# A two-layer graph network on one core: one more tile of lag in the delta stage, and every fourth message pair summed in two halves

## What is computed

```python
def step(S, x):
    qt, kt, vt, bt, gt = x
    S = S * jnp.exp(gt)[..., None, None]
    kv = jnp.einsum('bhk,ebhkv->ebhv', kt, S)
    delta = (vt[None] - kv) * bt[..., None]
    S = S + kt[None, :, :, :, None] * delta[..., None, :]
    ot = jnp.einsum('bhk,ebhkv->ebhv', qt * scale, S)
    return (S, ot)
```

```python
msg = jax.nn.relu(x[src] + edge_attr @ W_e + b_e)
aggr = jax.ops.segment_sum(msg, dst, num_segments=x.shape[0])
```

## Time and profile before

| | |
|---|---|
| time, median of 3 runs | 3208.61 us (3206.28 to 3215.51) |
| profiled execution | 3215.71 us, span 3213.9 us |
| PE busy | 2905.2 us, 90% |
| DVE busy | 1669.4 us, 52% |
| POOL busy | 1488.0 us, 46% |
| ACT busy | 1136.8 us, 35% |
| chain that ended last | PE 74%, issue 10%, DVE 5%, ACT 4%, POOL 4%, DMA 2% |

### The profile page before, as it was taken

The page is one execution under the profiler, slowest core; times in us unless marked ns, Lnnn a source line. Parts: engine busy times, 40 slices in busy tenths (PEclk is TensorE's granted clock), DMA queues, the critical chain, the costliest instruction groups (busy, mean ns, idle before and its releaser), DMA issues.

```text
span 3213.9 us, 46196 instructions
## 1 busy us (share of the span) xinstructions
PE 2905.2 (90%) x16081; PEld 1658.6 (52%) x16081; DVE 1669.4 (52%) x3820; ACT 1136.8 (35%) x2501; POOL 1488.0 (46%) x1471
## 2 busy tenths in 40 slices
PE   6999999988899899858989898999999999999828
PEld 3433566667676644447777664444533333444424
DVE  7633355578344432268777643442267777521361
ACT  3312422289122222346666441220044444331201
POOL 0565756488654537633333204545566666200004
PEclk9999999999999999979999998999999999999959
DMA  5400001120111234434454454211176666500404
GB/s 173 140 19 5 7 25 49 46 71 16 32 52 44 72 121 165 166 104 126 117 143 128 136 148 159 77 53 38 49 227 199 198 205 190 156 0 27 183 0 132
DMA packets 275961, 321.38 MB, mean 100 GB/s; under 512 B 155807, under 2 KB 193569, under 8 KB 275732
## 3 DMA queue, kind: packets, MB, share of 16 engines
q1 hardware_dynamic: 219684, 182.57, 18.7%
q0 software_dynamic: 51840, 134.60, 13.4%
q10 hardware_dynamic: 4208, 1.25, 0.2%
HBM read 215.75 MB, written 104.60 MB: 100 GB/s over the span
## 4 chain that ended last, share of the span: by engine, by line
PE 74%; issue 10%; DVE 5%; ACT 4%; POOL 4%; DMA 2%; SPq 0%; ACTq 0%; POOLq 0%; DVEq 0%
PE bank L2730 8%; PE bank L1522 5%; PE bank L2722 5%; PE bank L708 4%; PE bank L1301 4%; PE bank L2393 3%; PE bank L2884 3%; PE bank L2877 3%; PE bank L439 3%; PE bank L731 2%; PE bank L762 2%; PE bank L1117 2%; PE bank L2373 2%; PE bank L1311 2%; PE bank L858 2%
## 5 line engine op out<-in xcount | busy, mean ns | idle before, releaser
L2702 POOL DMA_INDIRECT conv_src<-xn_rows,keep x288 | 272.9, 948 | 175.7 <-DVE conv_msg L2768 110.4
L291 POOL DMA_INDIRECT sorted_bias<-perf_rec,place x256 | 259.7, 1014 | 146.0 <-PE bank L708 91.6
L2730 PE MATMUL bank<-conv_msg,conv_hot 128*128 128x512 f32 x576 | 273.0, 596 | 0.6 <-ACT conv_msg L2749 0.6
L2768 DVE TENSOR_TENSOR conv_msg<-bank,conv_src 128x512 f32<-128x512 f32 x288 | 185.5, 686 | 47.2 <-PE bank L2722 47.2
L1936 POOL TENSOR_TENSOR delta_dec<-delta_dec,rates_of 128x512 f32<-128x512 f32 x64 | 68.8, 1075 | 282.5 <-ACT delta_dec L1988 282.5
L666 POOL DMA_INDIRECT sorted_edge<-rec,place x128 | 127.1, 993 | 141.4 <-PE bank L1362 75.0
L2749 ACT ACTIVATE conv_msg<-conv_msg 128x1024 f32<-128x1024 f32 x144 | 152.0, 1056 | 102.0 <-DVE conv_msg L2768 102.0
L1117 PE MATMUL bank<-bias_prod,bias_hot 128*128 128x256 f32 x640 | 148.2, 387 | 25.1 <-ACT bias_hot L1070 13.0
L2722 PE MATMUL bank<-conv_we,conv_eT 64*128 64x512 f32 x576 | 164.5, 648 | 0.7 <-ACT conv_eT L2746 0.7
L1101 POOL TENSOR_TENSOR bias_prod<-bias_col,bias_rec 128x512 f32<-128x512 f32 x128 | 147.2, 1179 | 16.4 <-PE bank L1117 15.7
L1117 PEld LDWEIGHTS bank<-bias_prod,bias_hot 128*128 128x128 f32 x640 | 120.1, 192 | 53.7 <-issue 28.1
(11 more groups left out here) (502 smaller groups left out, 6674.8 us busy)
## 6 DMA issues: line engine op xcount, KB each, us to landing
keep<-slot_qkv SPq DMA_DIRECT2D x32, 512.0 KB, 4.0
delta_kv<-slot_qkv SPq DMA_DIRECT2D x32, 512.0 KB, 3.9
sorted_edge<-sort_pad SPq DMA_DIRECT2D x8, 1440.0 KB, 7.4
keep<-sorted_edge SPq DMA_DIRECT2D x18, 640.0 KB, 4.8
slot_out<-delta_o SPq DMA_DIRECT2D x64, 128.0 KB, 2.2
conv_src<-xn_rows,keep POOLq DMA_INDIRECT x288, 3.6
X<-in_x SPq DMA_DIRECT2D x4, 1024.0 KB, 11.3
sorted_bias<-perf_rec,place POOLq DMA_INDIRECT x256
```

Source lines behind the costliest of these rows:

```text
L291: POOL.indirect_dma_start(out=sorted_bias, out_offset=bass.IndirectOffsetOnAxis(ap=place[:, 0, c:c + 1], axis=0), in_=rec0[:, c, :], in_of ...
L2702: POOL.indirect_dma_start(out=src[:, n % 4, j, :], out_offset=None, in_=xn_rows, in_offset=bass.IndirectOffsetOnAxis(ap=rec[:, g % 3, k + ...
L2730: a = PE.matmul(bank[n % 2][:, :], hot[:, g % 2, k + j, :], msg[:, q, j, :], start=j == 0, stop=j == 1)
L2768: DVE.tensor_tensor(msg[:, q, j, :], bank[2 + 2 * q + j][:, :], src[:, n % 4, j, :], ALU.add).then_inc(*raw.up())
```

## The change

In the delta stage the ring of key products holds ten tiles instead of nine, and the main part, the import of the inverses, and the constants FIRST, ALONE and TWO all move two chunks (one tile) later. To make room, `kv` has two buffers instead of three, `o` three instead of four, `kd`, `r` and `w` one instead of two, and a table `strict` is dropped. Each smaller ring adds a wait on the step that last read the buffer. The chain of 30 columns is spread over 7.3 chunks instead of 5.4; a column has two plan entries now, and where its product falls ahead of `BA`, its update is placed behind `BA`. `L copy` moves from 6.33 to 8.23 chunks after the batch begins. From chunk 18 on the high mask is made by ACT in four activations, between `Z copy` and `U copy`, and no longer by POOL.

In the message stage pairs with n % 4 == 1 are summed in halves: relu writes an fp32r tile `high`, DVE computes `low` = relu(msg) - high, and PE sums with four fp32r matmuls (two of `high`, two of `low`) in place of two f32 ones. `raw` is one instruction of 128x1024 for both tiles. `turn`, `eT`, `edge`, `raw`, `relu` and `gather` stand earlier in the plan; `pack` and `hot` stay.

```diff
-            R = 9
+            R = 10
-            MID, MAIN = 15.8, 17.2
-            ALONE, TWO, FIRST = 16, 14, 16
+            MID, MAIN = 17.8, 19.2
+            ALONE, TWO, FIRST = 18, 16, 18
-            kv = sb("kv", [P, 3, 2, D])
+            kv = sb("kv", [P, 2, 2, D])
-            strict = sb("strict", [P, 32 * 32])
-            kd, r_, w = (sb(n, [P, 2, HG, HD]) for n in ("kd", "r", "w"))
-            o = sb("o", [P, 4, HG, HD])
+            kd, r_, w = (sb(n, [P, HG, HD]) for n in ("kd", "r", "w"))
+            o = sb("o", [P, 3, HG, HD])
...
-                return (("mask", -0.45), ("turn", -0.35), ("kq", -0.25), ("low mask", 0.17), ("gram", 0.22), ("decay", 0.25),
+                return (("high mask", -0.1), ("turn", -0.35), ("kq", -0.25), ("low mask", 0.17), ("gram", 0.22), ("decay", 0.25),
...
-                plan.append((2 * t + (14.6 if t >= 2 else 13.6 + 0.4 * t), "UL in", t))
-                plan.append((2 * t + MAIN - 3.0, "load kv", t))
+                plan.append((2 * t + (16.6 if t >= 2 else 13.6 + 0.4 * t), "UL in", t))
+                plan.append((2 * t + MAIN - 2.6, "load kv", t))
...
-                    at = 0.75 + (5.4 if q else 3.0) * (31 - k) / 31
+                    at = 0.75 + (7.3 if q else 3.0) * (31 - k) / 31
...
-                    plan.append((first + int(at) + part, "block column", (q, k)))
-                plan.append((first + (6.33 if q else 5.19), "L copy", q))
-                plan.append((first + (6.34 if q else 5.2), "blocks out", q))
+                    plan.append((first + int(at) + part, "block product", (q, k)))
+                    plan.append((first + int(at) + (0.745 if q and part < 0.7 else part), "block update", (q, k)))
+                plan.append((first + (8.23 if q else 5.19), "L copy", q))
+                plan.append((first + (8.24 if q else 5.2), "blocks out", q))
...
+                    if what == "high mask":
+                        ACT.wait_ge(*decay_sum.at(n))
+                        for i, h in enumerate(range(g * HG, (g + 1) * HG)):
+                            a = ACT.activation(dec_half[:, 0, i, :], const("upto"), AF.Copy, scale=rate_half[:, 0, t, h:h + 1])
+                        a.then_inc(*masked.up())
...
+            high, low = (sb(n, [P, 2, 2, D], F32H) for n in ("high", "low"))
...
+                return n % 4 == 1
...
-                for what, at in (("gather", -3.6), ("turn", -2.3), ("eT", -2.2), ("edge", -1.75), ("raw", -1.4), ("relu", -0.85),
+                for what, at in (("gather", -3.9), ("turn", -3.05), ("eT", -2.9), ("edge", -2.15), ("raw", -1.8), ("relu", -1.25),
                                  ("sum", 0.0), ("add", 0.6)):
                     plan.append((n + at, what, n))
+                if in_halves(n):
+                    plan.append((n - 0.7, "low", n))
...
                         for j in range(2):
-                            a = PE.matmul(bank[n % 2][:, :], hot[:, g % 2, k + j, :], msg[:, q, j, :], start=j == 0, stop=j == 1)
+                            PE.matmul(bank[n % 2][:, :], hot[:, g % 2, k + j, :], high[:, n // 4 % 2, j, :], start=j == 0, stop=False)
+                        PE.wait_ge(*lowered.at(n // 4 + 1))
+                        for j in range(2):
+                            a = PE.matmul(bank[n % 2][:, :], hot[:, g % 2, k + j, :], low[:, n // 4 % 2, j, :], start=False,
+                                          stop=j == 1)
                         a.then_inc(*summed.up())
...
-                        for j in range(2):
-                            DVE.tensor_tensor(msg[:, q, j, :], bank[2 + 2 * q + j][:, :], src[:, n % 4, j, :],
-                                              ALU.add).then_inc(*raw.up())
+                        DVE.tensor_tensor(msg[:, q, :, :], pairs[1 + q][:, :, :], src[:, n % 4, :, :], ALU.add).then_inc(*raw.up())
+                    if what == "low":
+                        DVE.wait_ge(*active.at(n + 1))
+                        if n >= 8:
+                            DVE.wait_ge(*summed.at(n - 7))
+                        DVE.scalar_tensor_tensor(low[:, n // 4 % 2, :, :], msg[:, q, :, :], 0.0, high[:, n // 4 % 2, :, :].bitcast(F32),
+                                                 ALU.max, ALU.subtract).then_inc(*lowered.up())
```

More of the change, by code:

```diff
@@ L1966, in scalar @@
                         continue
-                    if what not in ("kq", "low mask", "exp", "Z copy", "U copy", "Zb copy", "T copy", "w"):
+                    if what not in ("kq", "high mask", "low mask", "exp", "Z copy", "U copy", "Zb copy", "T copy", "w"):
                         continue
@@ L2168, in vector @@
                             DVE.wait_ge(*L_ready.at(n))
-                        DVE.scalar_tensor_tensor(flat(Us), flat(Bs), -1.0, strict[:, :], ALU.mult, ALU.mult
-                                                 ).then_inc(*blocks.up())
+                        DVE.tensor_scalar(flat(Us), flat(Bs), -1.0, None, ALU.mult).then_inc(*blocks.up())
                         DVE.wait_ge(*blocks.now())
                         DVE.memset(flat(Us)[:, 0:32 * 32:33], 1.0).then_inc(*blocks.up())
-                    if what == "block column":
+                    if what == "block product":
                         q, k = n
@@ L2699, in pool @@
                         if n >= 4:
[L2700 removed]
+                            POOL.wait_ge(*raw.at(n - 3))
                         for j in range(2):
```

84 lines of the change are left out of this document (48 added, 36 removed).

## The result

The changed kernel takes 3187.49 us, the median of 9 runs (3185.25 to 3200.14). The kernel before, in 9 runs beside them, takes 3208.61 us (3205.72 to 3219.67). The ratio is 0.9939, with a 95% interval of 0.9923 to 0.9954: 0.6% faster, 21 us where 10.6 were forecast. The profiled execution of the changed kernel took 3185.78 us with a span of 3183.9 us, 30 less than before.

What follows compares the result with a forecast made beforehand. PE bounds the message stage; DVE's order sets five or six of eight steady delta chunks, PE with ACT the rest. Message -16 and delta +5.5 make -10.5 from the 3208.6 median: 3198 us, range 3189 to 3208 (eight in ten 3175 to 3216).

Steps and rivals of the forecast that it cites:

- rival 1: Delta stage: the DVE-POOL lock is worth all 0.7 us of DVE per chunk, 15 us in all: 3183 us; chance 0.16.
- Rival 2: Message stage: the pack is in time, so 13.6 us of waiting are not lost: 3184 us; chance 0.15.
- the end of a batch: Delta stage: the chunk with the L copy takes 9.0 us, the next, late by the Bs load, 8.4.
- the half clock: Steady delta stage: about 2 of 65.6 us per eight chunks are half-clock stretches, left in before and after.
- The halves: Message stage: four fp32r matmuls of 0.22 us replace two f32 ones in 36 of 144 pairs: -30 us.
- DVE in the same time: Message stage: four pairs need 10.3 us of DVE plus 0.4 of gaps, PE 11.3, so `low` is hidden.
- Rival 3: Message stage: DVE becomes the bound, four pairs taking 11.7 to 11.9 us: 3201 us, or 3212 at 12.1; chance 0.15.
- The pack: Message stage: PE waits 0.8 us for the pack before a turn, at 17 of 18 packs: +13.6 us.
- The smaller rings: Delta stage: the new waits from fewer buffers cost nothing, covered by a chunk's 7 us.
- The high mask on ACT: Delta stage: four activations, 1.28 us, delay the U copy 0.2 to 0.3; an undisturbed chunk takes 7.3 us, not 7.06.
- Rival 4: Delta stage: ACT has no slack, the U copy is 0.55 us late in all 44 chunks: 3222 us; chance 0.12.
- The spread chain: Delta stage: a chunk amid an inversion, paced by a loop over DVE with 4.6 us of DVE work, takes 7.7 us.

Runs made afterwards that it cites:

- run 2: Changed kernel with the pack 0.4 of a pair earlier in the plan, ahead of the relu of pair 8g-2: 0.9893 of the kernel before.
- run 3: Changed kernel with the high mask back on POOL where it was: 0.9897 of the kernel before.
- run 1: Each half alone, the other stage's code as before: delta change alone 0.998 of the kernel before, message change alone 0.9937.
- run 9: Kernel before, unchanged, profiled once more on a third chip: 0.9997 against the other runs of the same kernel.
- run 6: Changed kernel with the columns over 5.4 chunks again, each product with its update, L copy at its old place: 1.0013 of the kernel before.
- run 4: The changed kernel, same file, on another chip: 0.9985 of the kernel before.
- run 8: Changed kernel with no pair summed in halves, new order and single raw kept: 1.0002 of the kernel before.

## Why the prediction was right, step by step

The total went the way that was forecast, and the time lies in the range given for eight in ten, 3175 to 3216. It lies 1.5 us below the forecast's own range, 3189 to 3208, and nearer to the 3183 and 3184 of rivals 1 and 2, whose mechanisms did not come. The gain forecast was half of what came. The message stage carries the result, and there the mechanism held. The delta stage was forecast 5.5 us slower and became faster: two of its terms, the end of a batch and the half clock, were off, so that part of the forecast failed, and the total has its direction from the message stage.

- **The halves.** Right. Two fp32r matmuls take 0.47 us, 0.235 each, where I took 0.22; 36 times 0.79 is 28, where I took 30. Without the pack's waits the stage is 29.5 us shorter (run 2).
- **DVE in the same time.** Right: it names itself nowhere as PE's releaser in that stage, and `low` took 1.22, not 1.53. Rival 3 is out.
- **The pack.** Right in place and cause, too high in price: 0.55 us at 17 packs, 9.6 by run 2, where I had 13.6. Relu started 0.1 to 0.2 earlier than I had it. Together the message stage gave 19.9 where I had 16. From the first sum it takes 416 us, not the 426 of the prediction's signs; 426 is 442 - 16, and 442 us was the stretch of the earlier trace rows, where the stage itself takes 434. Rival 2 is out; run 2 is what it would have been.
- **The smaller rings.** Right: in the stretch 1450 to 1800 POOL waits 39.0 us in 45 times before it writes `kd`, and no wait of PE names POOL, `r`, `w` or `kv`.
- **The high mask on ACT.** Right: 0.2 us of PE at each of 44 U copies, and an undisturbed chunk of 7.3 to 7.4. Rival 4 would have needed 0.5; it is out. Run 3 adds that the whole move costs 4.7 us, and that PE's waits for DVE grow by 7.4 with the mask back on POOL. So rival 1, which hoped for 15 more from the lock, is out too, although the time came near its 3183. Its sum was wrong as well: the forecast's W after the change has no lock in it, so what the rival could add is 0.7 - 0.4 = 0.3 us of DVE, half of it in P, 7 us. By the count of lengthened column operations the lock took 23.4 / 44 = 0.5 us of DVE in each chunk before, between the forecast's 0.4 and the rival's 0.7.
- **The spread chain.** Right in the number, half right in the mechanism: the six chunks beside the one with the L copy and the one behind it average (62.4 - 8.9 - 7.3) / 6 = 7.7, and P was 7.7. But P is a loop over DVE, and PE waits for DVE in 17 chunks of 44. Of the six, 7.6, 8.6 and 7.7 do so, and three of 7.4 don't; "chunks of 7.3 in the inversion" stood among the signs of being wrong. That the average met P is partly luck. The 8.6 is not explained by an average of columns.
- **The end of a batch.** Half right. The chunk with the L copy took 8.9, predicted 9.0 (the parts listed there give 0.3 + 1.3 + 0.8 = 2.4 without the copy and not 2.7, so by them it would have been 9.3). The next took 7.3, predicted 8.4: Bs was not late, since its load was issued early enough; waits for it sum to 1.0 us. That is 1.1 us in each of 5.5 batches, 6 us.
- **The half clock.** "About 2 of 65.6 are stretches at half clock that I leave in both": that failed. Before had two chunks of 11.5 us, each with a stretch at half clock, where the message part alone (run 1), with the same code there, has 8.5 and 8.0; the changed kernel had none. That is 6.5 us. Where they fall changes between executions: run 9 has one such chunk (11.3) and run 1 its first of 12.6. But each of the three profiles with the old lag has one or two, and in the steady stage of the eleven with the new lag no chunk takes over 10 us and none has half clock behind the second `solve`, with the spread chain or without (run 6). So the change seems to have a part in it, which no run shows. The two chunks in the profile of before, with granted clocks of 0.56 and 0.71:

```profile
1588.00:1599.50 11.50, 11.03 (x110) 9.22 (x110) 9.23 (x27) 4.36 (x13) 1.95 (x3) 0.56 0.42 105
1680.00:1691.50 11.50, 9.89 (x111) 8.06 (x111) 3.43 (x11) 4.94 (x15) 2.61 (x3) 0.71 0.66 184
```

- **The lag.** Right in cause, too low in price: `r` of chunk 0 at 1444.62, right at the end of `through`, where I had 1443, and 10.9 us where I had 7.5, within the bound of 13. Half clock in the filling was not counted (L2133 took 1.97 us).
- **The tail.** -2 predicted. The profile says -10, but that is a stretch at half clock again: the changed kernel and the delta part alone have the same code there, and took 141.1 and 150.8 (run 4), and 151.3 (run 1). The stretch 1860 to 1990 of the changed kernel, and of the delta part alone:

```profile
1860.00:1990.00 130.00, 111.74 (x1132) 72.19 (x1132) 45.21 (x142) 38.25 (x101) 39.74 (x39) 0.95 0.50 156
```

```profile
1860.00:1990.00 130.00, 112.47 (x1100) 75.87 (x1098) 41.89 (x134) 35.62 (x97) 34.54 (x35) 0.84 0.50 153
```

With 0.95 against 0.84 of the clock, 10 us come and go between executions. A pair of profiles can differ by that much from a pair of medians, as the 30 and the 21 us here.

Against the medians the delta part was forecast at +5.5, slower, and is about 6 faster (run 1, 2 to 11): the steady stage's term of 0 was the one that failed, by Bs and by the clock.

The lock that the prediction drew on is there, but taking it away is a gain only where DVE is the bound, and the chain's new places had taken most of it already; by run 3 the mask on POOL is the better one.

## What to carry to other kernels

When a step is moved ahead to feed a faster engine, list what each engine must have done before it: here one pack was left in its place, and 17 waits of 0.6 us took a third of what the halves gave; one number in the plan brought it back. Where a load has to be moved past the step that waits for it, count when its issue, not its step, comes, and a copy moved behind a critical one only shifts the wait if its store is in front of the next load. And time a change on more than one chip: this one is worth 0.6% on one chip and 0.15% on another, which is less than the 0.3% that a measurement of this kernel can tell from no change.

## What the runs showed of the hardware beyond that

- **DVE slows the issue of gathers on POOL.** Without `low` an issue takes 0.95 us (mean of 288), and the longest is 0.99 in the kernel before. With 36 `low` instructions of 128x1024 from SBUF to SBUF the mean is 1.01 and 45 take over 1.2 us, 29 of them while such an instruction runs; with 72 of them it is 1.16 and 93. `raw`, with one input in PSUM, lengthens no issue in run 8 (mean 0.95). But two inputs in SBUF are not enough: `hot`, a tensor_tensor with both in SBUF, overlaps 117 issues in run 8, and their mean is 0.95 too. The Trainium skill (SBUF — State Buffer, "Who interferes with whom") says that a DVE instruction with two inputs in SBUF contends with a GpSimd instruction that reads SBUF, and infers that a tensor_tensor leaves the writing of a DMA's descriptors alone; the issues beside `hot` agree. Beside `low`, a scalar_tensor_tensor with both in SBUF, issues are longer; what it holds up no run tells, and 16 of the 45 long issues don't overlap one.

```profile
L2713 POOL DMA_INDIRECT conv_src<-xn_rows,keep x288: 940/946/1792, 2318.8 to 2734.2; - x144
```

```profile
L2702 POOL DMA_INDIRECT conv_src<-xn_rows,keep x288: 942/947/988, 2331.4 to 2764.2; - x144
```

The first row is the changed kernel, the second the kernel before (min/median/max ns).

- **Chips differ, and most in the message stage.** The same kernel before took 3208.61, 3216.65, 3254.80 and 3252.11 us in four sets of runs. In all profiles what follows the message stage kept its length to 4 us (435.1 to 439.2), the part ahead of the delta stage took 1343 to 1348 in the first result and in runs 1 to 3 and 1367 to 1382 in the others, and the message stage of one and the same kernel 414.0 and 438.8. Whether the places where ACT and DVE start late come of the chip's transfers, and why there are more of them with the halves, stays open.
